# RWKV state stage in pairs of sequences, and another issue order in the local attention layer

## What is computed

```
def step(state, inp):                       # _wkv, scanned over the tokens of a sequence
    rt, kt, vt, wt = inp
    kv = kt[..., :, None] * vt[..., None, :]
    out = einsum('bhk,bhkv->bhv', rt, state + u * kv)
    return (state * wt[..., None] + kv, out)
```

## Time and profile before

| | us |
|---|---|
| median of 3 runs | 9200.64 (9198.53 to 9206.41) |
| the profiled execution, its time | 9209.76 |
| its span | 9208.0 |
| RWKV state stage, in it | two stretches of about 270, from 3842.7 and from 4718.7 |
| local layer's 24 turns, in it | 161.6 each; the first instruction of line 2640 at 5382.1, the 24th at 9098.1 |

### The profile page before, as it was taken

The page is one execution under the profiler, slowest core; times in us unless marked ns, Lnnn a source line. Parts: engine busy times, 40 slices in busy tenths (PEclk is TensorE's granted clock), DMA queues, the critical chain, the costliest instruction groups (busy, mean ns, idle before and its releaser), DMA issues. The chain is left out here.

```text
span 9208.0 us, 239595 instructions
## 1 busy us (share of the span) xinstructions
PE 7274.1 (79%) x90533; PEld 4218.8 (46%) x90713; DVE 6526.9 (71%) x14614; ACT 3000.1 (33%) x5686; POOL 3112.8 (34%) x3950
## 2 busy tenths in 40 slices
PE   5999999999747256568556688888888888888887
PEld 3666666666212122232233355545555455554544
DVE  8777777777574756745765477777777777777776
ACT  2111111111433132234223344444444444444444
POOL 1333333333000002200310155555555555555553
PEclk8999999999878667568656899999999999999999
DMA  0000000000000000000000311111111112112111
GB/s 19 1 0 0 0 0 0 0 0 0 5 0 15 0 0 0 1 1 0 0 1 1 108 51 50 53 57 50 50 58 53 48 53 57 50 51 57 48 53 59
DMA packets 156950, 243.06 MB, mean 26 GB/s; under 512 B 21616, under 2 KB 136848, under 8 KB 150160
## 3 DMA queue, kind: packets, MB, share of 16 engines
q1 hardware_dynamic: 155920, 228.84, 8.2%
HBM read 187.06 MB, written 13.66 MB: 22 GB/s over the span
## 5 line engine op out<-in xcount | busy, mean ns | idle before, releaser
L2700 POOL TENSOR_TENSOR big<-big 128x512 f32<-128x512 f32 x776 | 1044.4, 1377 | 324.7 <-DMA big<-norms 317.1
L2690 POOL TENSOR_TENSOR big<-big 128x512 f32<-128x512 f32 x388 | 495.0, 1276 | 1770.0 <-DVE big L2532 1770.0
L1805 POOL TENSOR_TENSOR small<-big 128x480 f32<-128x480 f32 (+14 forms) x240 | 220.4, 951 | 2185.2 <-ACT big L1563 1863.7
L2107 PE MATMUL banks<-hidden,big 128*128 128x256 f32 x3104 | 840.3, 405 | 112.7 <-DVE big L2532 39.5
L834 POOL TENSOR_TENSOR big<-big 128x128 f32<-128x128 f32 x1024 | 415.4, 406 | 1339.9 <-DVE big L780 1339.5
L600 ACT ACTIVATE banks<-banks 128x128 f32<-128x128 f32 x1024 | 268.3, 262 | 1823.7 <-DVE banks L763 1823.7
L334 PE MATMUL banks<-big,constants_on_chip 128*128 128x512 f32 (+15 forms) x1088 | 530.1, 640 | 357.8 <-DVE big L1696 191.5
L334 PE MATMUL banks<-big,weights_even 128*128 128x512 f32 (+5 forms) x1152 | 620.1, 691 | 235.1 <-DVE big L1086 45.2
L489 PE MATMUL banks<-big 128*128 128x256 f32 x2050 | 732.2, 439 | 61.9 <-ACT big L574 59.5
L2171 PE MATMUL banks<-big,hidden 128*32 128x512 f32 x6144 | 768.2, 599 | 4.1 <-ACT big L2422 4.1
L2150 PEld LDWEIGHTS banks<-big 32*32 32x32 f32 x49152 | 537.9, 103 | 424.7 <-issue 424.0
(11 more groups left out here) (349 smaller groups left out, 14635.4 us busy)
## 6 DMA issues: line engine op xcount, KB each, us to landing
big<-norms SPq DMA_DIRECT2D x776, 128.0 KB, 3.0
big<-qk SPq DMA_DIRECT2D x50, 512.0 KB, 4.9
big<-vo SPq DMA_DIRECT2D x25, 1024.0 KB, 6.3
weights_odd<-ffn SPq DMA_DIRECT2D x25, 537.5 KB, 5.5
hidden<-big SPq DMA_DIRECT2D x171, 64.0 KB, 4.1
hidden<-big SPq DMA_DIRECT2D x25, 256.0 KB, 3.7
hidden<-big SPq DMA_DIRECT2D x25, 255.8 KB, 4.5
big<-pairs SPq DMA_DIRECT2D x6, 1024.0 KB, 10.3
```

The costliest lines, as they stand in the source:

```text
L2107: mm = self.nc.tensor.matmul(bank[:, n * QTOK:(n + 1) * QTOK], u["w" + name.lower()][:, (2 * g + n) * P:(2 * g + n + 1) * P], u["xs"][:, a ...
L2690: self.nc.gpsimd.tensor_tensor(dst, cos, sin, ALU.add).then_inc(*e.did(("turned_pair", f, name, g)))
L2700: self.nc.gpsimd.tensor_tensor(x, x, u["norms"][:, n, g].unsqueeze(1).broadcast_to([P, 2, QTOK]), ALU.mult).then_inc(*e.did(("scaled", f, ...
```

## The change

It does two things.

The state stage runs over 16 units u in place of 32 tiles: unit u is tile j = u // 2 of a pair of sequences. Keys are copied by ACT from one bank (`kcopied`); DVE masks the values straight from PSUM into SBUF (`masked`); PE makes the contributions with one matmul for each head and sequence (64 columns of keys by 512 of values), so that they lie in PSUM by head; DVE steps the two states alternately, with the contribution as a PSUM operand; PE reads a unit out as soon as it is stepped. Two sets of buffers alternate. Transposes run one unit ahead, reading out one unit behind.

The second part changes the order in which the local layer's functions are called on PE, ACT, DVE and POOL, moves `exps` and `normalise` of the second half into the next quarter, and gives the Gelu table one load for three calls.

```diff
+def state_buffers(core):
+    b = core.b
+    ring = [b[6][:, n * 2048:(n + 1) * 2048].rearrange("p (s c v) -> p s c v", s=BATCH, v=HS) for n in range(2)]
+    return dict(
+        keys=core.bank[0], values=core.bank[1:3], contrib=[core.bank[3:5], core.bank[5:7]], read=core.bank[7],
...
+def pair_of(u):
+    return u // 2, (2 * (u % 2), 2 * (u % 2) + 1)
...
 def rwkv_tensor(core, e):
...
+        def transposes(u):
...
+            if u:
+                pe.wait_ge(*e.after(f"{r}kcopied", u - 1))
+            if u >= 2:
+                pe.wait_ge(*e.after(f"{r}masked", u - 2))
+            for n, s in enumerate(pair):
+                a = s * SEQ + j * P
+                nc.tensor.transpose(keys[:, n * P:(n + 1) * P], b[3][:, a:a + P], ident)
+                mm = nc.tensor.transpose(values[:, n * P:(n + 1) * P], b[4][:, a:a + P], ident)
+        def contributions(u):
+            pe.wait_ge(*e.after(f"{r}kcopied", u))
+            pe.wait_ge(*e.after(f"{r}masked", u))
+            if u >= 2:
+                pe.wait_ge(*e.after(f"{r}stepped", u - 2))
+            for n in range(2):
                 for h in range(2):
+                    rows = slice(HS * h, HS * h + HS)
+                    mm = nc.tensor.matmul(u_["contrib"][u % 2][n][rows, :], u_["kT"][u % 2][:, n, rows],
+                                          u_["own"][u % 2][n][:, :, rows], start=True, stop=True, skip_group_check=True)
+        def read_out(u):
...
+            pe.wait_ge(*e.after(f"{r}stepped", u))
+            if u:
+                pe.wait_ge(*e.after(f"{r}joined", u - 1))
...
+        for u in range(PAIRS):
+            if u + 1 < PAIRS:
+                transposes(u + 1)
+            contributions(u)
+            if u:
+                read_out(u - 1)
+        read_out(PAIRS - 1)
...
 def rwkv_vector(core, e):
...
+        def mask(u):
+            dve.wait_ge(*e.after(f"{r}turned", u))
+            if u >= 2:
+                dve.wait_ge(*e.after(f"{r}contrib", u - 2))
+            for n in range(2):
...
+                tt(u_["own"][u % 2][n], values.unsqueeze(1).broadcast_to([P, PER_TILE, P]),
+                   core.c("own_chunk").unsqueeze(2).broadcast_to([P, PER_TILE, P]), ALU.mult).then_inc(
+        def step(u):
+            dve.wait_ge(*e.after(f"{r}contrib", u))
+            if u >= 2:
+                dve.wait_ge(*e.after(f"{r}read", u - 2))
+            for k in range(PER_TILE):
+                for n, s in enumerate(pair):
...
+                    dve.wait_ge(*e.after(f"{r}state", s, c - 1))
+                    stt(u_["state"](s, c), u_["state"](s, c - 1), core.small2[:, at:at + 1], new, ALU.mult,
+                        ALU.add).then_inc(*e.did((f"{r}state", s, c)))
+        def join(u):
+            dve.wait_ge(*e.after(f"{r}read", u))
...
+            tt(out, out, read, ALU.add).then_inc(*e.did((f"{r}joined", u)))
+        for u in range(PAIRS):
+            mask(u)
+            if u >= 2:
+                join(u - 2)
+            if u:
+                step(u - 1)
+        join(PAIRS - 2)
+        step(PAIRS - 1)
+        join(PAIRS - 1)
...
 def local_tensor(core, e):
-            for g in range(3):
-                t.project(f, "K", g)
-            t.attend((f - 1) % QUARTERS, 1)
-            t.project(f, "K", 3)
+            t.project(f, "K", 0)
+            t.project(f, "K", 1)
             t.value(f, 0, 0)
             t.value(f, 0, 1)
+            t.project(f, "K", 2)
+            t.project(f, "K", 3)
+            t.score_masks(f, 0)
+            t.score(f, 0, 0)
+            t.score(f, 0, 1)
+            t.score(f, 0, 2)
+            t.attend((f - 1) % QUARTERS, 1)
+            if f == 1:
+                t.mean(0)
+            t.score(f, 0, 3)
             t.sums(f, "K")
...
 def local_vector(core, e):
-            for name in NAMES:
-                for g in range(GROUPS):
-                    v.rope(f, name, g)
-                v.guard(f, name)
+            v.rope(f, "K", 0)
+            v.normalise((f - 1) % QUARTERS, 1)
+            v.rope(f, "K", 1)
+            v.rope(f, "K", 2)
+            v.rope(f, "K", 3)
+            if f == 1:
+                v.centre(0)
+            v.guard(f, "K")
             v.lower(f, 0)
+            v.rope(f, "Q", 0)
+            v.rope(f, "Q", 1)
+            v.rope(f, "Q", 2)
+            v.guard(f, "Q")
+            v.rope(f, "Q", 3)
+            v.normalise(f, 0)
...
-            v.normalise(f, 1)
...
 def local_pool(core, e):
+            p.add(f, "K", 0)
+            p.add(f, "K", 1)
+            p.add(f, "K", 2)
+            p.add(f, "Q", 0)
+            p.add(f, "K", 3)
+            p.add(f, "Q", 1)
+            p.add(f, "Q", 2)
             p.keep_last(f)
+            p.add(f, "Q", 3)
...
```

More of the change, by code:

```diff
@@ L2177, in attend @@
         e, pe, u = self.e, self.pe, self.u
+        pe.wait_ge(*e.after("turned", q, jj))
         if e.layer == "local":
[L2179 to L2181 removed]
+            pe.wait_ge(*e.after("kept", q, jj, 3, **({"back": 1} if jj and q == QUARTERS - 1 else {})))
             if jj == 0:
@@ L2312, in entry_vector @@
         e.name_last("folded", d, "vector")
+    for k in range(2 * (SUBS * QUARTERS) - 5, 2 * (SUBS * QUARTERS)):
+        nc.vector.memset(u["slots"][k % SLOTS], 0.0).then_inc(*e.did())
+    dve.wait_ge(*e.after("stored", DEPTH - 1))
+    nc.vector.memset(u["prob"][1].rearrange("p c k -> p (c k)"), 0.0).then_inc(*e.did())
     e.leave()
@@ L2408, in exps @@
         e, act = self.e, self.act
-        act.wait_ge(*e.after("lowered", f, jj))
+        if e.layer == "local":
+            act.wait_ge(*e.after("lowered", f, jj, **({"back": 1} if jj and f == QUARTERS - 1 else {})))
         p = self.u["prob"][jj].rearrange("p c k -> p (c k)")
@@ L2759, in exit_scalar @@
         a.ffn_inverse(h)
+    core.nc.scalar.preload_act_table(ACT.Gelu)
     for h in range(HALVES):
-        a.gelus(h, range(3))
+        for k in range(len(IC)):
+            a.gelu(h, k)
+    core.nc.scalar.preload_act_table_set(LN_EXP)
     core.to_act.restart("out")
```

271 lines of the change are left out of this document (124 added, 147 removed).

## The result

The changed kernel takes 8661.44 us (median of 4 runs, 8650.97 to 8669.91) against 9203.06 for the one before in the same job: ratio 0.9411, 95% interval 0.9395 to 0.9428, so 542 us less where 674 had been forecast. The profiled execution has a span of 8665.6, 542.4 less than before. It splits exactly: 326.6 less up to the first L2707 (the twin of L2640, once a turn, at the start of its quarter 3; it starts at 5055.5 in place of 5382.1), 222.9 less in the 23 turns from there to the last L2707, and 7.1 more behind it.

The account below looks back on a forecast made before the run. No engine bounded the state stage, PE and DVE waiting in turn; in the local loop PE was busy 141.7 of 161.6. From 9209.8, less 295 (state stages) and 377 (loop), 8538, or 8529 against the median; range 8410 to 8760.

Parts of the forecast that it names:

- the clash of DVE and POOL: Local loop, rival at 0.2: each `normalise` multiply loses 1.06 beside POOL's scaling, 8.5 a turn, 204 in all, giving 8733.
- the signs of being wrong: PE's largest loop wait above 5 a turn, POOL's scaling ending a masks' wait in every quarter, or a stage over 150.
- the rival in which the halves of 64 columns don't overlap: State stage, chance 0.12: a unit's contributions take 7.2 instead of 3.6 at the low clock, 99 more, giving 8628.
- the 7.0 a unit: State stage: time per two-sequence tile, taken between 6.1 (DVE the bound) and 7.8; 16 units plus 11 make 123.
- the full-clock rival: State stage, chance 0.1: PE runs at full clock, its 7.8 becomes 3.9, DVE bounds the unit with 6.1; 29 less, 8500.
- the walk: Local loop, counted from a quarter's first key projection: `turned` ready at 7.4, PE reaching `attend` at 8.0, so the 12.4 wait goes.
- The wait of 2.5 that the walk gave for K3's bank: Local loop, quarter 2: DVE comes late from quarter 1, so K3's bank waits some 2.5 in place of today's bank waits.
- The masks' walk: Local loop, short quarter: queries scaled at 34.8, quarter 28 to 29 long, so PE waits about 1 for POOL, once a turn.
- the other 7.5 of PE's idle time: Local loop: PE's idle time per turn besides the 12.4 wait for `turned`, left as large as it was, in new places.
- `attend(f, 0)` "comes about when `turned` does": Local loop, end of the walk: this `attend` was said to come about when `turned` is ready; no wait size was given.
- the wait coming back elsewhere: Local loop, rival at 0.07: `attend(f, 0)`, K3's bank or the Gelus take over the removed wait; only the state stage gains, 8906.
- The slower rival through POOL and the norms: Local loop, chance 0.03: masks wait for the last `scale`, 28.8 a quarter; slower overall above 43.5, doubled way and scalings giving 9621.

Follow-up runs that it names:

- spread: The changed kernel with PE's projections, values and sums placed between the scores at the start of a quarter; 8565.88 us, ratio 0.9319 to the kernel before.
- local_only: The kernel before with the new order of the local layer alone; 9006.43 us, ratio 0.9797.
- state_only: The kernel before with the new state stage alone; 8819.57 us, ratio 0.9593.

## Why the prediction was right, and where it was off

The time fell inside the range, in its upper half, 132 above the forecast. Part of that is luck: the state stages gave 29 more than forecast and the local layer 158 less, and the two errors are of opposite sign. The range held because it was drawn wide for the clash of DVE and POOL; the forecast's own part of it ended at 8640, and its turns at 150. Of the signs of being wrong one came true: PE's largest wait in the loop is 6.2 a turn (142.6 / 23, issue at the scores), above the 5 that was named, so for the loop the mechanism was right for the wait that went, and wrong for what was left. The multiply at 1.79, outside 1.2 to 1.4, and `attend`s of 3.15, 3.51 and 3.60 (in the three turns from 7000), of which none was to be left, speak the same way. The terms by the profiled execution:

| term | forecast | measured |
|---|---|---|
| two state stages | -295 | 541 to 106.8 + 110.4: -324 |
| turns of the loop | 24 x 15.7 = -377 | 9.7 each, in the 23 that were measured -223 |
| the rest up to the first L2707 (three quarters of a turn, and the entry) | in the row above | -3 |
| behind the last L2707 (the last quarter, and the exit) | 0 to +5 | +7.1 |

**State stage: right, 29 undersized.** The steps stand 0.19 apart (forecast 0.20), two masks take 2.35 (2.4), the addition 0.42 (0.4), eight contribution records 3.6 to 3.7 at the low clock (3.6), so the rival in which the halves of 64 columns don't overlap is out. The read-out is 2.65 or less, not 3.2. DVE's unit is 5.7, where I had summed 6.1 (the terms as I wrote them, 2.4, 3.2 and 0.4, add up to 6.0): instructions overlap by a tenth here and there. The term that was mis-sized is the 7.0 a unit, chosen from between the engines' bounds with a clock taken from the stage before, 0.58; it measured 6.0 to 6.25. The granted clock was 0.77 and 0.73; the full-clock rival, at 0.1, came about half way. The Trainium skill (TensorE: Matmul & The Clock Gate, "What's actually happening") has activity releasing the clock; the trace agrees in part, since PE is now busy 87% of the first window against 66% and the granted clock rose from 0.58, and yet units at either level follow each other (3861.26 and 3867.36 above).

**Loop: the wait went as forecast, the turn didn't.** From the walk, `turned` would be there in time, and it is: 12.4 to 0.1 a turn. The slow `attend`s went only in part: PE's busy time fell by 2.0 a turn and not by 3.3. The wait of 2.5 that the walk gave for K3's bank didn't come; the waits for banks are down to 1.1 a turn (L2694). The masks' walk was right too, in that they hardly wait for POOL, yet stand so near to it that the 1.6 later `guard` makes them wait 2.7 a turn. The sentence that failed is "I leave the other 7.5 of PE's idle time as large as it is, in new places". It became 12.7, and PE's busy time 139.1 (forecast 138.4); together the 6.0 a turn that are missing. Of these:

- Issue waits went from 2.3 to 7.3 (the earlier trace rows show the largest of before); I had read them as a constant of the work. They are a property of the order: PE runs out of instructions in dense runs of scores, and goes on 1.2 to 1.7 us after the next block has landed. The three scores in a row were there before as well, but behind an `attend` that had waited; that this wait gave the supply time to run ahead fits, and wasn't tested by itself. `spread` takes 5.8 of the 7.3 away, and 3.6 a turn.
- `attend(f, 0)` "comes about when `turned` does" was the right walk with the wrong label: it also needs `added`, which DVE issues behind `normalise`, in quarter 1 behind `centre` and `norm`. This is 3.5 a turn. I had listed what each step moves past, but not what `attend(f, 0)` waits for at the end of DVE's queue.
- The clash of DVE and POOL, a rival at 0.2, did come about in part. I priced it at 1.06 on each of eight multiplies; the mean went up 0.44, 3.5 a turn. The norm's first instruction fell by 0.45, and all of DVE's busy time rose only from 121.9 to 122.6 a turn: much of the clash was there before. It acts through the lateness of `added`, and it is not apart from the item above: with POOL's scaling nearly gone that wait falls to 1.3.

"DVE's 125 busy leave room", said against the wait coming back elsewhere, was the wrong reading of a mean: DVE is busy 122.6 of 151.9 and still late at the end of two quarters of four, while it stands waiting at `guard` (315.3 us in all).

The slower rival through POOL and the norms needed 43.5 a quarter; nothing came near it. `exps` and the Gelu tables cost nothing that shows. The stretch behind the loop's last L2707 is 7.1 longer, and 6.8 in `local_only` but only 0.2 in `state_only`, so it belongs to the local change; I had costed its extra softmax at 0 to 5, and the cover was not there.

**Open.** Why the old loop behind the new state stage has a turn of 158.58 and behind the old stage 161.57, and why the parts add up to 567 alone and 542 together. Of the 69 us, 28 are PE's busy time; 17.5 are its wait for `turned`, 288.7 to 271.2; 16.4 are `mean`'s wait for a DMA, 17.6 to 1.2; and 5.6 are issue waits. In that loop the norm's instruction took 1329 ns against 1528 and the multiply 1325 against 1358, so DVE and POOL meet at other moments; that is a description, and no run tells what sets it.

## What to carry to other kernels

When a long wait of the bounding engine is taken away, don't carry the rest of its idle time over as a constant: sort it by cause, ask which of it the wait had been covering, and look at each consumer's whole list of waits and at what stands in front of each releaser in its queue. Where a wait is called "issue", hold its end against the landings of the instruction blocks. Runs of many very short matmuls are best broken up by larger ones, which costs only the order. And follow a fix once round the loop before making it: four of five further reorderings here moved a wait to the next engine and gained nothing.

## What was not expected of the hardware

- PE stops for up to 2.5 us inside runs of 32-by-64 matmuls with no other engine to wait for, and goes on 1.2 to 1.7 us after a 16384-byte block of instructions has landed, at every one of 983 stops. 168 us in 23 turns became 35 with the same instructions in another order and 247 in a denser one, and shifting the loop by 21 matmuls moved the stops to other instructions without changing their sum.
- Eight float32 records with 128 rows, 64 columns of weights and 512 moving columns take 3.68 at the 1.2 GHz level and 1.94 at 2.4 GHz. At the lower level that is 0.46 a record, half of the 0.9 of full-width ones and as forecast: the two column halves work beside each other.
- While POOL scales, a DVE multiply of 1024 columns goes from 1.22 to over 2 us, which the earlier trace rows had shown; new is that the norm's `tensor_scalar` of 512 columns, with one input in SBUF, goes from 0.49 to 1.38.
- DVE's scalar-tensor-tensor with 64 columns: 0.19 apart when each depends on the last but one, 0.31 when on the last.
